# A transposing matmul that carries 48 columns of weights instead of 128, in an attention and mixture-of-experts kernel

## The reference, cut to what matters

```python
q = (decoded @ Wq.T + bq)   # 16 heads of 16; k and v from the context likewise
qk = jnp.einsum('bhqd,bhkd->bhqk', q, k)
attn = jax.nn.softmax(qk, axis=-1)
z = jnp.einsum('bhqk,bhkd->bhqd', attn, v)
# ... residual, layer norms, router, top 2 of 8 experts:
hid = jax.nn.gelu(jnp.einsum('bth,ehf->btef', z, W1) + b1, approximate=False)
outs = jnp.einsum('btef,efh->bteh', hid, W2) + b2
```

## Time and profile before

| | us |
|---|---|
| median of 3 runs | 848.51 |
| lowest and highest | 848.0, 851.65 |
| the profiled execution, its own time | 848.51 |
| span of the profiled execution, first to last instruction | 846.7 |
| TensorE busy | 750.9 |
| VectorE busy | 652.2 |
| POOL busy | 550.9 |
| ScalarE busy | 536.9 |

### The profile page before, as it was taken

How to read it: one execution, slowest core, us unless ns; L and a number is a source line. 1 busy time by engine, 2 the same in 40 slices (tenths; PEclk the granted TensorE clock), 3 DMA queues, 4 the chain that set the end, 5 groups by cost and what they waited for, 6 DMA issues and landing times.

```text
span 846.7 us, 26240 instructions
## 1 busy us (share of the span) xinstructions
PE 750.9 (89%) x8056; PEld 589.6 (70%) x8057; DVE 652.2 (77%) x1828; ACT 536.9 (63%) x1412; POOL 550.9 (65%) x610
## 2 busy tenths in 40 slices
PE   3489999999999999999999997665787798999994
PEld 1356777777777777777777775444686797999994
DVE  7389999898999998998989998893567864555562
ACT  3236788888888888888878885443363354555551
POOL 6323877877877778778778684343654466777773
PEclk9599999999999999999999999755998899999997
DMA  8846567677677686776776857612233234443441
GB/s 194 154 119 137 128 151 166 157 173 166 154 177 165 147 187 143 175 164 154 175 170 148 196 126 195 185 21 47 44 66 51 38 57 66 67 69 51 67 64 19
DMA packets 152791, 104.43 MB, mean 123 GB/s; under 512 B 68656, under 2 KB 147852, under 8 KB 152608
## 3 DMA queue, kind: packets, MB, share of 16 engines
q1 hardware_dynamic: 132598, 77.03, 40.0%
q0 software_dynamic: 11776, 16.15, 11.8%
q10 hardware_dynamic: 8362, 10.57, 4.3%
HBM read 36.65 MB, written 17.33 MB: 64 GB/s over the span
## 4 chain that ended last, share of the span: by engine, by line
PE 70%; DVE 12%; DMA 7%; issue 5%; POOL 3%; SPq 1%; DVEq 1%; ACT 1%; ACTq 0%; POOLq 0%
PE pj L863 10%; PE pj L832 9%; PE s_row L877 9%; PE s_row L968 9%; PE zt L909 9%; PE s_t L897 8%; PE pj L979 4%; PE zt L979 3%; PE pj L850 3%; DVE negmax L1334 3%; DMA out_x<-index_space,idx_s 2%; DMA q_stack<-q_part 2%; PE tr L917 1%; PE tr L933 1%; PE pj L956 1%
## 5 line engine op out<-in xcount | busy, mean ns | idle before, releaser
L1334 DVE TENSOR_REDUCE negmax<-s_row 100x1 f32<-100x361 f32 x512 | 251.4, 524 | 29.4 <-PE s_row L877 24.4
L1156 ACT ACTIVATE p_t<-s_t 128x400 f32<-128x400 f32 x384 | 189.1, 503 | 52.4 <-PE s_t L897 43.2
L877 PE MATMUL s_row<-stack_x,q_stack 125*128 125x361 bf16 x512 | 132.8, 320 | 13.9 <-DVE negmax L1334 5.6
L703 POOL DMA_INDIRECT out_x<-index_space,idx_s x57 | 93.3, 1638 | 74.7 <-DVE index_space L1442 35.0
L897 PE MATMUL s_t<-q_stack,stack_x 128*128 128x100 bf16 x1536 | 128.3, 211 | 9.8 <-ACT p_t L1156 8.8
L897 PEld LDWEIGHTS s_t<-q_stack,stack_x 128*128 128x128 bf16 x1536 | 93.8, 99 | 53.9 <-issue 27.0
L968 PE MATMUL s_row<-w_qkv,v_aug 128*128 128x128 f32 x912 | 118.9, 286 | 11.4 <-DVE v_aug L1429 11.1
L968 PEld LDWEIGHTS s_row<-w_qkv,v_aug 128*128 128x128 f32 x912 | 112.5, 201 | 14.4 <-DVE v_aug L1429 13.0
L1339 DVE TENSOR_SCALAR p_t<-p_t 128x1200 f32<-128x1200 f32 x128 | 102.7, 802 | 6.8 <-ACT p_t L1156 5.6
L863 PE MATMUL pj<-w_qkv,ct 128*128 128x256 f32 x384 | 107.4, 403 | 0.2 <-ACT k_rest L1084 0.2
L1142 ACT ACTIVATE w_qkv<-s_row,b_k 128x128 f32<-128x128 f32 x228 | 65.3, 369 | 66.2 <-PE s_row L968 63.2
(11 more groups left out here) (234 smaller groups left out, 1435.7 us busy)
## 6 DMA issues: line engine op xcount, KB each, us to landing
stack_x<-k_part SPq DMA_DIRECT2D x192, 192.0 KB, 3.8
q_stack<-q_part SPq DMA_DIRECT2D x186, 64.0 KB, 2.0
ct<-in_ctx_t SPq DMA_DIRECT2D x32, 361.0 KB, 4.9
stack_x<-in_w ACTq DMA_DIRECT2D x8, 512.0 KB, 6.3
w_s<-in_w ACTq DMA_DIRECT2D x14, 256.0 KB, 3.0
zscr<-zn SPq DMA_DIRECT2D x32, 100.0 KB
z_in<-zscr SPq DMA_DIRECT2D x32, 100.0 KB
zf_d<-zf_s SPq DMA_DIRECT2D x32, 100.0 KB
```

Of the source, the lines that this page charges most:

```text
L703: pool.indirect_dma_start(out_rows[0:n], bass.IndirectOffsetOnAxis(idx_s[:, k.slot:k.slot + 1], 0), ys[:, k.slot, :], None, bounds_check=n ...
L877: nc.tensor.matmul(s_row[h % 2][:, 0:KEYS], q_stack[0:MROW, b.slot, h, :], k_stack[0:MROW, b.slot, h, 0:KEYS], start=True, stop=True).then ...
L1156: nc.scalar.activation(p_t[:, quad % 2, kt, :], s_t[g % 2][:, 0:4 * Q], ACT.Exp).then_inc(exp_done, 1)
L1334: v.tensor_reduce(negmax[:, b.slot, h:h + 1], s_row[h % 2][0:Q, 0:KEYS], AXIS.X, ALU.max, negate=True).then_inc(max_done, 1)
```

## The change

`m_rows` is 48 columns wide instead of 128. The transposing matmul takes these 48 columns as weights and writes 48 rows of `tr` instead of 128. The memset of the other columns and the wait for it are gone. What ScalarE copies from `tr` was 48 rows before and still is.

```diff
-            m_rows = sb(att, "m_rows", [Q, 128], BF16)
+            m_rows = sb(att, "m_rows", [Q, 3 * H], BF16)
...
                     if b.known and b.index == 0:
                         pe.wait_ge(ident_ready, 1)
-                        pe.wait_ge(pad_written, 4)
                     wait_bank_free(tr_users, "max", b)
-                    nc.tensor.matmul(tr[:, 0:Q], m_rows[:], ident_bf[:], start=True, stop=True).then_inc(mt_done, 1)
+                    nc.tensor.matmul(tr[0:3 * H, 0:Q], m_rows[:], ident_bf[:], start=True, stop=True).then_inc(mt_done, 1)
...
-                v.memset(m_rows[:, 3 * H:], 0.0).then_inc(pad_written, 1)
```

## The result

The changed kernel takes 852.45 us (median of 22 runs, 849.64 to 855.98), the kernel before 847.63 us (22 runs beside them, 841.58 to 855.48): 1.0054 times as long, with a 95% interval from 1.0036 to 1.0074. The prediction was 853.3 us, and slower by over 0.5% was its likeliest outcome. The interval lies clear of no change, but it does not settle on which side of 0.5% the kernel is. The medians differ by 4.8 us, the size of its sum, but single executions of the same kernel scatter by several us, so the agreement to a tenth is luck. The traces have to say whether the reasons hold.

What follows compares the result with a forecast made beforehand. TensorE was taken to bound the attention loop, each narrow transpose costing 0.21 us: 14 x 0.21 + 13 x 0.14 = 4.8 us, five transposes free, 848.5 + 4.8 = 853.3 us. The 8-in-10 range was 849.5 to 856.5 us.

Steps and rivals of the forecast that it cites:

- Way in: Before each narrow transpose, behind the L877 pair: the change of tile costs 0.09 us, start at 0.40 instead of 0.31.
- Way out: Behind each narrow transpose, at L897: leaving the narrow tile costs 0.10 us, priced from L897 behind L909.
- the load laid open: At each transpose: weight load no longer covered by earlier matmuls, between 0 and 0.106 us, taken as 0.02.
- Where L897 came late by TensorE's queue: Seven batches, 165.2 to 443.6 us: queue gap of 0.07 us behind the transpose absorbs part, 0.14 us left each.
- Where VectorE's maximum held the next pair: Six batches, like that at 428 us: next L877 pair's wait of 0.07 us swallows part, 0.14 us left each.
- The full ones: 14 batches of the attention loop with neither queue gap nor maximum wait: the whole 0.21 us each.
- The early ones: Loop's beginning: the third transpose and that at 118.70 us counted free behind waits, ordinary ones at 0.21 us.
- The rest, at nothing: Removed memset and pad_written wait, later maxima, buffers 160 bytes lower: 0 us, half a microsecond either side for the range.
- The free switch: Rival at the transpose: a single matmul in a 64-wide tile pays no price, time stays 848.5 us; chance 0.17.
- The gain from a shorter load: Rival at the transpose: load on the path and falling with columns, 1.9 us gained, 846.6 us; chance 0.04.
- The load laid open wholly: Rival at the transpose: 0.106 us exposed instead of 0.02, 2.3 us more, 855.6, up to 858 us; chance 0.09.
- More swallowed than counted: Rival in the loop: 27 batches each lose another 0.07 to 0.14 us to later waits, 849.5 to 851.4 us; chance 0.08.

Runs made afterwards that it cites:

- base: Kernel before with one edit in GpSimd's expert stage, the scatter wait count loaded with stated bounds; 0.9997 times before's time, loop distance 434.53 us.
- w64: base with the transpose reading 64 of the 128 columns of m_rows (tile 128x64); 1.0082 times before's time, loop distance 439.23 us.
- filler: Changed kernel plus an unused 80-column buffer behind m_rows, so later buffers keep their old addresses; 1.0049 times before's time, distance 438.95 us.
- adjacent: Changed kernel plus a second 48-column matmul, result unused, right behind the transpose; one run, 852.71 beside 850.13 us, distance 439.11 us.
- t32: Changed kernel with the transpose cut into two matmuls of 32 and 16 columns, tile 128x32; one run, 851.73 beside 850.13 us, distance 438.66 us.
- w72: base with the transpose reading 72 of the 128 columns of m_rows (tile stays 128x128); 1.0024 times before's time, distance 434.43 us.
- extra48: base plus an unused 48-column matmul (tile 128x64) before the third head's scores in each batch; 1.0084 times before's time, distance 440.36 us.
- extra100: base plus an unused 100-column matmul (tile 128x128) before the third head's scores in each batch; 1.0002 times before's time, distance 435.89 us.

## Why the prediction was right

**What bounds the kernel.** Right. Time put on TensorE in the loop came out at the end: 4.33 us in the loop, 4.8 between the medians, whose interval (0.36 to 0.74% of 847.63, 3.1 to 6.3 us) holds both. One reading was short: the chain's stay on VectorE at 437.67 us is two maxima, not one, 1.0 us in all. It is 1.0 us after, too, so VectorE moved with TensorE and swallowed nothing.

**The price of one transpose.** Right in its size. Way in: 0.09 us forecast, 0.40 - 0.31 = 0.09 found. Way out, 0.10 forecast, and the load laid open, 0.02: in the trace L896 starts 0.16 - 0.05 = 0.11 us later, and the matmul is 17 ns longer (225 against 208). The matmul's length holds the load, so the two sum to what the forecast had, to 0.01: 0.20 us found, 0.21 forecast. The choice of 0.02 rather than 0.106 for the load was the one that could have gone wrong by 2.3 us, and that it came out is partly luck. Its reason was that L909's matmuls hardly differ among themselves (247 and 249 ns). But the narrow transpose's don't either (224 to 226 ns), and each of them is 17 ns longer than a wide one: a part that every matmul pays can't be seen in their spread.

**What stays on the path.** First to 30th transpose: 450.34 us before (55.70 to 506.04), 454.75 after (52.45 to 507.20), 4.41 more. The forecast for it is the 4.8 us less the 0.12 that the 30th pays behind its start, some 4.6. For the last two transposes, which were counted at nothing, the traces can't decide: from the 30th to the 32nd it is 32.28 us before and 33.00 after, but 32.77 in base and 32.15 in w64. Of the kinds of batches:
- Where L897 came late by TensorE's queue (0.14 forecast): it costs 0.11 to 0.14. The gap behind that transpose was 0.12 and is 0.15.
- Where VectorE's maximum held the next pair (0.14 forecast): 0.11 to 0.13. The pair of before at 429.31 us took 0.56 us, after at 429.82 it takes the usual 0.47; in the chain its share fell from 0.39 to 0.31. The wait is gone, as the forecast had it.
- The full ones (0.21 forecast): in the six that come every third batch from the 9th to the 24th 0.28 on average, 0.22 to 0.34, **a term that was too small by 0.07**. (Of the others, the 27th and 29th show 0.21, the 7th 0.12 and the 28th 0.09.) The surplus isn't at the transpose. It lies in the last value group of that batch, which takes 0.91 us at 426.19 (above) where before it took, in TensorE's order of time:

```profile
425.95 0.84 PE L909 MATMUL zt<-p_t,v_aug 128*32 128x100 f32 x24
```

  Other such groups take 0.72 or 0.73 us. The longer one goes with the narrow transpose: in each of the five kernels with one in this place (after, w64, filler, adjacent, t32) it takes 0.90 us or more about once in three batches, in before, base and w72 it takes 0.80 to 0.94 and is missing in some turns, and in extra48, where the narrow matmul stands elsewhere, it is missing entirely. Why it is longer is open; no experiment was made on it.
- The early ones, from the 2nd transpose to the 7th: 0.37 us in sum, where the forecast has 0.63, three at 0.21 and two free. (The free ones are the 4th, at 103.01 us, and the 5th, at 118.70; the earlier trace rows and the prediction count them one too low.) The waits of the beginning swallowed more than I had counted.

The last two errors have opposite signs. Three batches late in the loop take 46.4 us before and 46.9 after, as forecast, because the 0.07 too little in one stands against 0.01 to 0.02 too much in each of the two others. So the total of 4.8 was near 4.4 by terms of which two partly cancelled.

**The rest, at nothing.** Right: filler shows it for the addresses; for the memset and the wait w64 does, which keeps both and costs 4.70 us against base, no less than after.

**The rivals.** The free switch fell with the gaps of 0.40 and 0.16 us. The gain from a shorter load fell twice: the load isn't shorter (99 ns), and w72 shows a longer load, 109 ns, costing nothing. The load laid open wholly fell with 17 ns. More swallowed than counted happened in the early batches, for some 0.3 us, not the 1.9 us of that case.

**The range.** 849.5 to 856.5 us held the median, and the interval of the ratio, taken times 848.5, goes from 851.6 to 854.8.

## What to carry to other kernels

A matmul whose output has 64 rows or fewer, alone between full-width ones, cost this kernel's TensorE 0.1 us on each side, whatever it saved in columns. Zeros up to the next tile were free (72 and 128 columns gave the same loop), and a second narrow matmul next to the first was free as well, so narrow ones that must be there are best put next to each other. Before moving one next to the others, look at who waits for what it moves past: here the move cost about three times what it could save. And where single executions scatter by more than the effect, measure in the trace from one instruction of the bounding loop to another, not by the span or a fixed window.

## What the runs showed of the hardware

**A weight load of 16 columns takes nearly as long as one of 72, and 72 take longer than 128.** By the rows of each kernel's LDWEIGHTS of the transpose (median ns): 128 columns 96, 72 columns 109, 64 columns 106, 48 columns 99; t32's parts 92 with 32 columns and 85 with 16. From 16 to 72 columns that is about 78 ns and 0.44 ns for each column. The 100 columns of the identity in extra100 take 125 ns, near the same line, which gives 122; 128 columns lie far below it. The Trainium skill (TensorE: Matmul & The Clock Gate, Weight-path perf modes — Fast Weight Load (FWL) and DoubleRow) says of a fast weight load that it is used with all 128 columns when the type isn't FP32; the trace agrees, 96 ns against 109 for 72 columns and 125 for 100. Between matmuls of wide tiles the loads were hidden under the matmuls before them, and their length changed no time.

**What a narrow tile lays open grows with the columns, as the load does.** The matmul of 100 moving columns takes 208 ns in a wide tile, and 211, 218, 225 and 232 with 16, 32, 48 and 64 weight columns in a narrow one: 7 ns for 16 columns, on 204. The loads grow by the same 7 ns (85, 92, 99, 106), which is why I read the surplus as a part of the load.

**A tile 64 wide and one 32 wide cost the same to enter and to leave** (0.40 and 0.15 to 0.16 us in after, w64 and t32). I had expected that what L909 pays might come from its four matmuls side by side.

**Executions of this kernel start unevenly.** The transfer in the chain at some 26 us took 16.04 us in one execution and 12.10 in the other, and the runs of one kernel lie up to 14 us apart (841.58 to 855.48 for before). A difference of 0.5% shows in the loop of a single trace, and in the total only over many runs.
